# Graph kernel: out-degree sums moved between passes, rows of T in an area of their own, the last group's linear steps ahead of pass six

## The chip, the core and the metric

The kernel runs on one core of a Trainium2 chip. The metric is the time on the device in microseconds; lower is better. TensorE is called PE here, VectorE DVE, ScalarE ACT, GpSimd POOL, and SyncE SP; SP's instructions here are nearly all DMA issues.

## What is computed

Four graph layers in a row on 6250 nodes with 128 features and 200000 edges (src, dst), each followed by `x = layernorm(x + layer(x))`:

```python
# layer 0, three times (l = 0, 1, 2), relu between
t = x @ W[l].T + b[l];  x = (t + segment_sum(t[src], dst)) * 0.5
# layers 1 and 2: GCN with self loops; layer 2 with prelu
out = segment_sum(norm[:, None] * (x @ W)[src], dst) + b
# layer 3: attention over edges, batch norms over all edges
hihj  = concat(x[src], x[dst])
exp_e = exp(silu(bn(hihj @ Wf + bf)));  we = weight[src] * exp_e
a = we / segment_sum(we, dst)[dst]
z = silu(bn(einsum('ed,hdk->ehk', hihj, Wg) + bg))
h = segment_sum(a * z, dst);  out = bn(h) + x
```

The batch norms over edges in layer 3 need sums over the edges of `T[src] + Q[dst]` and of its square (T and Q are x times the two halves of W3, which holds Wg and Wf). They follow from the count of edges for each pair of nodes, and one term needs the out-degree of each node: how many edges start there (`odeg`).

## The kernel before

The nodes are 49 blocks of 128 rows. The kernel counts edges once into a matrix A of counts in device memory (`counts_d`): 49 blocks of target nodes by 49 blocks of source nodes. A word holds two counts: its upper half one of source blocks 0 to 24, its lower half one of source blocks 25 to 48. All segment sums of the layers 0 to 2 are then products with A, in **passes**. Passes one (`FIRST`) and six (`LAST`) go by single blocks (`mm`), with loads called AB, two halves to a block. Passes two to five are grouped (`GROUPED`): 13 groups (`GRP`), ten of 4 target blocks and three of 3.

For each group A comes in seven **chunks** (`CHUNKS`): six of 4 source blocks and a seventh of one. A chunk of a group of four is 1024 KB, of a group of three 768 KB. Three buffers `CA` take the chunks in turn, so that the load of chunk n waits until chunk n-3 is read by all its readers: PE (`chunk_used`), ACT (`chunk_expanded`), which turns the lower halves into floats in `CB`, and DVE, where a sum is taken (`chunk_summed`). The loads are issued by SP in order; `held` and `sums_read` are the counts it waits for. PE goes `highs(0) highs(1) lows_of(0) highs(2) lows_of(1) ... highs(6) lows_of(5)`, each a lot of 8 products (2 for `highs(6)`). The work on the group before stands in between: after `lows_of(0)` the linear step (`group_linear`, L1011), and in pass five also `group_turn` (L1018) and `group_tq` (L1024, products with W3, whose result is T and Q).

**DVE** takes the **out-degree sums**: `chunk_sums` adds up the upper or lower halves of a chunk (TENSOR_REDUCE, L1329) and adds the result to `odeg` (L1330). The table `OD` says in which pass which chunk's halves are summed: for each pass the chunks of the upper halves, then those of the lower halves. Chunks 0 to 2 of the upper halves are summed in pass one. For a group DVE does the sums of chunks 0 and 1, then `finish_group` of the group before (from L1362, L1364 or L1369: bias, relu or layer norm, and `group_split` into a high part, L1338, and the rest, L1340), then the sums of chunks 2 to 6, then in pass five `finish_rows` of the group before.

**Rows of T.** In pass five `finish_rows` writes the rows of T (`TRG`) and Q (`QTG`). TRG shares its place in `TMP` with `YG`, where `finish_group` writes y. POOL copies the high part into HS (L645), then issues the DMAs of T's rows to `table_d` (L647) and Q's to `q_d` (L648), waits for both, and counts `rows_out`. DVE waits for `rows_out` in `finish_group` ahead of y.

**Last group.** The linear step, turn and W3 products of group 12 of pass five stand within block 0 of pass six, ahead of its source blocks 4, 30 and 36. When the rows of group 12 are out, POOL starts the **gather**: for each of 1563 tiles of 128 edges it fetches the rows of T of their source nodes (L662), four sets of 16 tiles in `GS`, and writes them to `rows_d`. The edge loop reads these from there, and stands behind pass six, whose blocks from the third on need Q (`q_in`).

## Time and profile before

| | |
|---|---|
| median of 3 runs | 5065.88 us (5056.94 to 5069.64) |
| the profiled execution | 5055.68 us, its span 5053.8 us |
| PE busy | 3910.6 us, 77% |
| DVE busy | 3272.7 us, 65% |
| ACT busy | 2563.6 us, 51% |
| POOL busy | 1810.3 us, 36% |
| passes two to five | 1417.08 to 2729.6 us of the span |
| gather | 2758.3 to 4921.5 us |

The busy shares are means over stages in which different engines set the pace; what a part costs has to be read in its own stage. All times below are microseconds from the start of the span.

### The profile page before, as it was taken

The numbers are of one execution on the slowest core, as the hardware profiler recorded it, in microseconds if no ns is written. First come the engines' busy times: TensorE is split into PE (matmuls) and PEld (weight loads), VectorE is DVE, ScalarE is ACT, GpSimd is POOL, SyncE is SP. The second block draws the span as 40 slices with busy tenths as digits, with TensorE's granted clock in tenths as the row PEclk, the third lists the DMA queues.
The fourth block names the chain that finished last, engine by engine and source line by source line (L and its number), as shares of the span: only waits on it lengthen the run. The fifth ranks groups of instructions, "written<-read, shape, count | busy, mean of one in ns | idle before, by whom it ended". The sixth has DMA issues, their size and how long they took to land.

```text
span 5053.8 us, 99631 instructions
## 1 busy us (share of the span) xinstructions
PE 3910.6 (77%) x26349; PEld 3254.1 (64%) x26350; DVE 3272.7 (65%) x10813; ACT 2563.6 (51%) x5122; POOL 1810.3 (36%) x1839
## 2 busy tenths in 40 slices
PE   4666555569999989999997996888766666666775
PEld 2222222249988877889887996777755566666764
DVE  6999988775566555322332446888656667666777
ACT  1356788774444434445443444665534444444544
POOL 1000000000000000000002777777777777777770
PEclk8887877689999999999998998999878888888987
DMA  2011222247777766788887996777666666666762
GB/s 83 39 65 78 91 91 104 91 158 258 259 247 266 257 227 219 234 269 265 264 263 219 368 379 199 210 213 210 185 178 181 177 180 192 180 173 181 198 188 90
DMA packets 440519, 976.38 MB, mean 193 GB/s; under 512 B 55380, under 2 KB 159244, under 8 KB 421436
## 3 DMA queue, kind: packets, MB, share of 16 engines
q1 hardware_dynamic: 371619, 755.43, 45.6%
q0 software_dynamic: 67168, 218.56, 14.8%
q8 instruction: 55, 0.90, 0.1%
q10 hardware_dynamic: 1593, 0.80, 0.1%
q14 instruction: 84, 0.69, 0.0%
HBM read 777.04 MB, written 197.54 MB: 193 GB/s over the span
## 4 chain that ended last, share of the span: by engine, by line
POOL 32%; PE 32%; DVE 17%; issue 12%; DMA 3%; ACT 3%; ACTq 1%; SPq 1%; DVEq 0%; POOLq 0%; PEldq 0%; PEld 0%
POOL E L662 31%; PE banks L1040 21%; DVE F L1255 8%; PE banks L967 6%; DVE F L1256 6%; DMA CA<-counts_d 2%; PE banks L938 2%; POOL rows_d L673 1%; ACT banks L710 1%; PE banks L1011 1%; ACT stage L723 1%; PE banks L1072 1%; DMA q_d<-small 1%; ACT stage L721 1%; DMA E<-table_d,IX 1%
## 5 line engine op out<-in xcount | busy, mean ns | idle before, releaser
L662 POOL DMA_INDIRECT E<-table_d,IX x1563 | 1632.3, 1044 | 479.8 <-issue 474.0
L938 PE MATMUL banks<-F 128*128 128x392 bf16 x2368 | 621.1, 413 | 400.1 <-DVE F L1256 255.2
L1123 PE MATMUL banks<-E 128*128 128x129 bf16 x5424 | 427.0, 232 | 516.1 <-DVE E L1493 513.0
L1255 DVE TENSOR_SCALAR F<-F,front 128x392 bf16<-128x392 f16 x2368 | 732.7, 309 | 77.1 <-PE banks L938 70.1
L781 ACT ACTIVATE CB<-CA 128x2048 fp32r<-128x2048 uint16 (+1 forms) x312 | 558.6, 1811 | 392.8 <-DMA CA<-counts_d 371.0
L938 PEld LDWEIGHTS banks<-F 128*128 128x128 bf16 x2368 | 270.4, 114 | 750.8 <-issue 707.3
L1123 PEld LDWEIGHTS banks<-E 128*128 128x128 bf16 x5424 | 349.7, 103 | 585.5 <-DVE E L1493 579.9
L1040 PE MATMUL banks<-CA,HS 128*128 128x512 f32 (+1 forms) x2600 | 646.5, 392 | 47.5 <-DMA CA<-counts_d 47.5
L1040 PE MATMUL banks<-CB,HS 128*128 128x512 f32 (+1 forms) x2496 | 619.6, 388 | 3.3 <-ACT CB L781 3.3
L1040 PEld LDWEIGHTS banks<-CA,HS 128*128 128x128 f32 x2600 | 486.7, 192 | 142.2 <-DMA CA<-counts_d 48.5
L845 ACT ACTIVATE E<-E 128x130 f32<-128x130 f32 x1808 | 574.9, 392 | 0.5 <-DVE E L1527 0.5
L1256 DVE TENSOR_SCALAR F<-F,front 128x128 bf16<-128x128 f16 x2368 | 571.6, 241 | 0.0
L1128 PE MATMUL banks<-E,ident 128*128 128x129 f32 x3616 | 560.7, 302 | 11.5 <-DVE E L1512 10.2
L1135 PE MATMUL banks<-E 128*128 128x130 f32 x3616 | 527.7, 293 | 33.2 <-ACT E L845 33.2
L1040 PEld LDWEIGHTS banks<-CB,HS 128*128 128x128 f32 x2496 | 469.4, 192 | 87.1 <-ACT CB L781 4.0
L1135 PEld LDWEIGHTS banks<-E 128*128 128x128 f32 x3616 | 487.5, 208 | 43.5 <-issue 43.4
L634 POOL CAST HS<-TMP 128x128 f32 (+1 forms) x49 | 20.8, 425 | 1354.7 <-DVE TMP L1271 1354.7
L645 POOL CAST HS<-TMP 128x512 fp32r<-128x512 f32 (+3 forms) x52 | 56.4, 1084 | 1253.3 <-DVE TMP L1338 1253.3
L1128 PEld LDWEIGHTS banks<-E,ident 128*128 128x128 f32 x3616 | 490.2, 210 | 20.2 <-DVE E L1512 19.5
L830 ACT ACTIVATE E<-banks 128x516 f32<-128x516 f32 x452 | 271.4, 601 | 327.8 <-PE banks L1128 309.1
L1493 DVE TENSOR_SCALAR E<-E,node 128x512 bf16<-128x512 uint16 x452 | 194.8, 431 | 358.1 <-DMA E<-dst_d 301.0
L721 ACT ACTIVATE stage<-banks 128x400 f32 (+1 forms) x392 | 249.7, 637 | 342.9 <-PE banks L938 307.9
(235 smaller groups left out, 5296.2 us busy)
## 6 DMA issues: line engine op xcount, KB each, us to landing
CA<-counts_d SPq DMA_DIRECT2D x240, 1024.0 KB, 5.2
E<-rows_d SPq DMA_DIRECT2D x452, 260.0 KB
rows_d<-E POOLq DMA_DIRECT2D x99, 1040.0 KB
AB<-counts_d SPq DMA_DIRECT2D x98, 832.0 KB
counts_d<-stage SPq DMA_DIRECT2D x49, 1600.0 KB, 5.2
AB<-counts_d SPq DMA_DIRECT2D x98, 768.0 KB
E<-dst_d SPq DMA_DIRECT2D x452, 128.0 KB
CA<-counts_d SPq DMA_DIRECT2D x72, 768.0 KB, 4.9
```

What stands on the lines that cost most here:

```text
L662: g.indirect_dma_start(GS[:, t % (GSET * GSETS), :], None, table_d, bass.IndirectOffsetOnAxis(ap=IX[:, t:t + 1], axis=0)).then_inc(g_in[k] ...
L721: act.activation(high16[:, half, :, 2 * k * WIN:2 * (k + 1) * WIN].rearrange("p a h (u d) -> p u (a h) d", u=2), pair[:, :, 0:WB, :], ACT. ...
L781: act.activation(low(q, g, c)[:, 0:size], t[:, 0:size].bitcast(u16).rearrange("p (f k) -> p f k", k=2)[:, :, 0], ACT.Copy).then_inc(chunk_ ...
L845: ins = act.activation(MS[:, h, k, :], ZS[:, h, k, :], ACT.Copy, scale=we[:, h, k:k + 1])
L938: pe.matmul(banks_f[:, ds(e[k], HJ)], ol[:, c * CH + k, :], oh[:, c * CH + k, :], start=False, stop=True, skip_group_check=True).then_inc( ...
L967: ins = pe.matmul(agg[par][:, 0:wide], w, HS[u][:, s, 0:wide], start=(s == 0), stop=(s == NB - 1))
L1040: ins = pe.matmul(sums[:, 0:k * P].rearrange("p (k d) -> p k d", k=k), HS[u][:, s, h * P:(h + 1) * P], words(t, k, w)[:, :, j, :], start=( ...
L1123: ins = pe.matmul(o, OHT[:, k, :], QS[:, p, 0:EDG], start=(k & 1 == 0 and p == 0), stop=False, skip_group_check=True)
L1128: ins = pe.matmul(o, ident[:, :], PAs[:, h, k, :], start=False, stop=(k & 1 == 1), skip_group_check=True)
L1135: ins = pe.matmul(bank[:, 0:ROW], OH[:, h, k, :], MS[:, h, k, :], start=False, stop=True, skip_group_check=True)
L1255: ts(oh[:, n % RING, :], io16, KUL[:, 0, n:n + 1], None, ALU.is_equal)
L1256: ts(ol[:, n % RING, :], io16[:, 0:P], KUL[:, 1, n:n + 1], None, ALU.is_equal).then_inc(onehot_made, 1)
```

## The change

1. Table `OD`: pass two sums the lower halves of chunks 0, 1 and 2 (before: 0, 1), pass three those of 4 and 5 (before: 2 to 5), pass four that of 3 (before: none). The upper halves stay as they are (3 to 6 in pass two).
2. TRG moves from TMP to the start of `small`, over weights and biases of layer 0 that pass five doesn't read; the weights W12 and the biases bias0 change places for that. The wait for `rows_out` moves from `finish_group` to `finish_rows`.
3. POOL issues the two DMAs first and copies the high part into HS after that. Ahead of the gather it also waits for the last split (`group_low_made`), since GS lies over `small`.
4. PE does linear step, turn and W3 products of group 12 ahead of pass six, and no longer within it; ACT does the square root and the copy of the turned X ahead of the first expansion of pass six.

```diff
--- before.py
+++ after.py
@@ -48,7 +48,7 @@
 NLOW = NR // CW
 FIRST, LAST = 1, 6
 GROUPED = (2, 3, 4, 5)
-OD = {2: ((3, 4, 5, 6), (0, 1)), 3: ((), (2, 3, 4, 5)), 4: ((), ()), 5: ((), ())}
+OD = {2: ((3, 4, 5, 6), (0, 1, 2)), 3: ((), (4, 5)), 4: ((), (3,)), 5: ((), ())}
 assert NLOW * CW == NR and GRP[-1][0] + GRP[-1][1] == NB and 6 * CW * 4 * P <= (WB + NR) * 2 * P
 MASK = 4095
 EPS = 1e-5
@@ -109,9 +109,9 @@
         DTG = sb("DTG", [P, 2, NTP], u16)
         IX = sb("IX", [P, NT], u32)
         W0r = small[:, 0:3 * P].rearrange("p (l d) -> p l d", l=3)
-        W12 = small[:, 3 * P:5 * P].rearrange("p (l d) -> p l d", l=2)
+        W12 = small[:, 6 * P:8 * P].rearrange("p (l d) -> p l d", l=2)
         W3 = sb("W3", [P, 2 * EDG], f32)
-        bias0 = small[:, 5 * P:8 * P].rearrange("p (l d) -> p l d", l=3)
+        bias0 = small[:, 3 * P:6 * P].rearrange("p (l d) -> p l d", l=3)
         rowb1 = small[:, 8 * P:11 * P].rearrange("p (l d) -> p l d", l=3)
         biasQ = sb("biasQ", [P, EDG], f32)
 
@@ -128,7 +128,7 @@
         TOPG = TMP[:, 4 * P:4 * P + 4 * EDG]
         YT = TMP[:, 8 * P + 4:9 * P + 4]
         YG = TMP[:, 8 * P + 4:12 * P + 4]
-        TRG = TMP[:, 8 * P + 4:8 * P + 4 + 4 * ROW].rearrange("p (k f) -> p k f", k=4)
+        TRG = small[:, 0:4 * ROW].rearrange("p (k f) -> p k f", k=4)
         QTG = small[:, 11 * P:11 * P + 4 * EDG].rearrange("p (k f) -> p k f", k=4)
         ident = sb("ident", [P, P], f32)
         identr = sb("identr", [P, P], f32r)
@@ -642,14 +642,17 @@
                 w = EDG if q == 5 else P
                 for n, (b0, k) in enumerate(GRP):
                     g.wait_ge(group_top_made, group_no(q, n) + 1)
-                    g.tensor_copy(HS[q & 1][:, b0:b0 + k, 0:w], TOPG[:, 0:k * w].rearrange("p (k f) -> p k f", k=k)).then_inc(group_high_made, 1)
                     if q == 5:
                         g.dma_start(table_d.rearrange("(b p) f -> p b f", p=P)[:, b0:b0 + k, :], TRG[:, 0:k, :]).then_inc(t_row_out, 16)
                         g.dma_start(q_d[b0:b0 + k, :, :].rearrange("b p f -> p b f"), QTG[:, 0:k, :]).then_inc(q_row_out, 16)
+                    g.tensor_copy(HS[q & 1][:, b0:b0 + k, 0:w], TOPG[:, 0:k * w].rearrange("p (k f) -> p k f", k=k)).then_inc(group_high_made, 1)
+                    if q == 5:
                         g.wait_ge(t_row_out, n * 16 + 16)
                         g.wait_ge(q_row_out, n * 16 + 16)
                         g.sem_inc(rows_out, 1)
             g.wait_ge(idx_made, 1)
+            g.sem_inc(gate_g, 1)
+            g.wait_ge(group_low_made, len(GROUPED) * NGRP)
             g.sem_inc(gate_g, 1)
 
             def gather(n):
@@ -814,9 +817,9 @@
                     if p[0] == 5:
                         x_copied(p[1])
             copied(5, NGRP - 1)
-            expand(side(LAST, 0), turn_no(LAST, 0))
             root(5, NGRP - 1)
             x_copied(NGRP - 1)
+            expand(side(LAST, 0), turn_no(LAST, 0))
             expand(side(LAST, 1), turn_no(LAST, 1))
             expand(side(LAST, 0), turn_no(LAST, 0) + 1, order(LAST, 0) + 2)
             with act.Fori(0, NB // 2 - 1) as i:
@@ -1101,9 +1104,10 @@
                     pe.wait_ge(group_high_made, group_no(5, g) + 1)
                 return wait
 
-            pe.wait_ge(group_copied, len(GROUPED) * NGRP - 1)
-            mm(LAST, 0, side(LAST, 0), turn_no(LAST, 0), {0: last_rows(NGRP - 3), 4: lambda: group_linear(5, NGRP - 1), 30: lambda: group_turn(NGRP - 1),
-                                                         36: lambda: group_tq(NGRP - 1), GRP[-2][0]: last_rows(NGRP - 2), GRP[-1][0]: last_rows(NGRP - 1)})
+            group_linear(5, NGRP - 1)
+            group_turn(NGRP - 1)
+            group_tq(NGRP - 1)
+            mm(LAST, 0, side(LAST, 0), turn_no(LAST, 0), {0: last_rows(NGRP - 3), GRP[-2][0]: last_rows(NGRP - 2), GRP[-1][0]: last_rows(NGRP - 1)})
             with pe.Fori(0, NB // 2) as i:
                 for u in (1, 2):
                     mm(LAST, pe.snap(i * 2 + u), side(LAST, u), i + turn_no(LAST, u), {})
@@ -1363,8 +1367,6 @@
                     v.wait_ge(group_lin_done, n + 1)
                     link(tt(y, r, sums, ALU.add))
                 else:
-                    if q == 5 and g:
-                        v.wait_ge(rows_out, g)
                     v.wait_ge(group_lin_done, n + 1)
                     link(tt(y, sums, across(dinv, b0, k), ALU.mult))
                 v.sem_inc(group_lin_read, 1)
@@ -1400,6 +1402,8 @@
 
                 b0, k = GRP[g]
                 v.wait_ge(group_tq_done, g + 1)
+                if g:
+                    v.wait_ge(rows_out, g)
                 cpr(TRG[:, 0:k, EDG:ROW], wn[:, b0:b0 + k].unsqueeze(2))
                 tt(QTG[:, 0:k, :], psQ[:, 0:k, EDG:2 * EDG], along(biasQ[:, :], k, EDG), ALU.add)
                 link(cpr(TRG[:, 0:k, 0:EDG], psQ[:, 0:k, 0:EDG]))
```

On DVE, the second group of pass two (group 1, with the finishing of group 0), before. CA0, CA1 and CA2 are the three buffers; the sums behind the split (L1340) are those of chunks 3, 4, 5 and of the short chunk 6:

```order
L1364 TENSOR_TENSOR TMP<-TMP,banks 128x512 [waits group_lin_done,link_v]
L1372 TENSOR_SCALAR TMP<-TMP 128x512 [waits link_v]
L1338 TENSOR_SCALAR TMP<-TMP 128x512 [waits group_high_made,link_v]
L1340 TENSOR_TENSOR HS0_50<-TMP 128x4x128 [waits group_top_made]
L1329 TENSOR_REDUCE od1<-CA1_56 128x4 [waits chunk_summed,chunk_in1]
L1330 TENSOR_TENSOR odeg<-odeg,od1 128x4 [waits link_v]
L1329 TENSOR_REDUCE od1<-CA2_57 128x4 [waits chunk_summed,chunk_in2]
L1330 TENSOR_TENSOR odeg<-odeg,od1 128x4 [waits link_v]
L1329 TENSOR_REDUCE od1<-CA0_55 128x4 [waits chunk_summed,chunk_in0]
L1330 TENSOR_TENSOR odeg<-odeg,od1 128x4 [waits link_v]
L1329 TENSOR_REDUCE od1<-CA1_56 128x1 [waits chunk_summed,chunk_in1]
L1330 TENSOR_TENSOR odeg<-odeg,od1 128x1 [waits link_v]
```

And after (L1333 is L1329 of before, L1344 L1340):

```order
L1368 TENSOR_TENSOR TMP<-TMP,banks 128x512 [waits group_lin_done,link_v]
L1374 TENSOR_SCALAR TMP<-TMP 128x512 [waits link_v]
L1342 TENSOR_SCALAR TMP<-TMP 128x512 [waits group_high_made,link_v]
L1344 TENSOR_TENSOR HS0_50<-TMP 128x4x128 [waits group_top_made]
L1333 TENSOR_REDUCE od1<-CA0_55 128x4 [waits chunk_summed,chunk_in0]
L1334 TENSOR_TENSOR odeg<-odeg,od1 128x4 [waits link_v]
L1333 TENSOR_REDUCE od1<-CA1_56 128x4 [waits chunk_summed,chunk_in1]
L1334 TENSOR_TENSOR odeg<-odeg,od1 128x4 [waits link_v]
L1333 TENSOR_REDUCE od1<-CA2_57 128x4 [waits chunk_summed,chunk_in2]
L1334 TENSOR_TENSOR odeg<-odeg,od1 128x4 [waits link_v]
L1333 TENSOR_REDUCE od1<-CA0_55 128x4 [waits chunk_summed,chunk_in0]
L1334 TENSOR_TENSOR odeg<-odeg,od1 128x4 [waits link_v]
```

Behind the split there now stands a sum over chunk 2, and those over 3, 4 and 5 follow it.

On PE, the end of pass five and the start of pass six, before; L1040 is the grouped products, L967 those of pass six:

```order
L1011 MATMUL banks<-small_52,TMP 128x128 [waits group_lin_read,group_copied]
L1011 MATMUL banks<-small_52,TMP 128x128 x2
L967 MATMUL banks<-HS1_51,AB_53 128x258 x8
L967 MATMUL banks<-HS1_51,AB_53 128x258 [waits low_expanded]
L967 MATMUL banks<-HS1_51,AB_53 128x258 [waits a_in3]
L967 MATMUL banks<-HS1_51,AB_53 128x258 x10
L967 MATMUL banks<-HS1_51,AB_53 128x258 [waits low_expanded]
L967 MATMUL banks<-HS1_51,BX_54 128x258 x5
L1018 MATMUL banks<-ident,X 128x128 [waits group_x_ready]
L1018 MATMUL banks<-ident,X 128x128 x2
L967 MATMUL banks<-HS1_51,BX_54 128x258 x6
L1024 MATMUL banks<-W3,TMP 128x258 [waits group_xt_copied]
```

And after (L1014, L1021 and L1027 are L1011, L1018 and L1024 of before; L970 is L967):

```order
L1043 MATMUL banks<-CB2_60,HS0_50 128x384 x2
L1014 MATMUL banks<-small_52,TMP 128x128 [waits group_lin_read,group_copied]
L1014 MATMUL banks<-small_52,TMP 128x128 x2
L1021 MATMUL banks<-ident,X 128x128 [waits group_x_ready]
L1021 MATMUL banks<-ident,X 128x128 x2
L1027 MATMUL banks<-W3,TMP 128x258 [waits group_xt_copied]
L1027 MATMUL banks<-W3,TMP 128x258 x2
L970 MATMUL banks<-HS1_51,AB_53 128x258 [waits group_high_made,a_in2,group_low_made,agg_read]
L970 MATMUL banks<-HS1_51,AB_53 128x258 x11
L970 MATMUL banks<-HS1_51,AB_53 128x258 [waits low_expanded]
```

The three steps of group 12 now stand together ahead of the first product of pass six.

## Rows read from the trace of the kernel before

**Rows 1.** The page, chain of work that ended last: shares of the span by line.

```profile
POOL E L662 31%; PE banks L1040 21%; DVE F L1255 8%; PE banks L967 6%; DVE F L1256 6%; DMA CA<-counts_d 2%; PE banks L938 2%; POOL rows_d L673 1%; ACT banks L710 1%; PE banks L1011 1%; ACT stage L723 1%; PE banks L1072 1%; DMA q_d<-small 1%
```

**Rows 2.** The gather's line: count, min/median/max ns, first and last start.

```profile
L662 POOL DMA_INDIRECT E<-table_d,IX x1563: 940/947/6478, 2758.3 to 4921.5; - x196
```

**Rows 3.** Passes two, three, four: length, busy of PE, PEld, DVE, ACT, POOL, PEclk, DMA.

```profile
1417.08:1727.76 310.68, 304.19 (x1471) 258.85 (x1469) 197.57 (x229) 149.65 (x94) 13.91 (x14) 0.99 0.78 261
1727.76:2092.91 365.15, 326.82 (x1471) 274.83 (x1471) 195.80 (x331) 149.99 (x104) 14.09 (x13) 0.93 0.67 221
2092.91:2393.85 300.94, 300.94 (x1472) 257.50 (x1472) 79.35 (x237) 148.00 (x105) 14.06 (x13) 1.00 0.80 267
```

**Rows 4.** Waits of the load queue, pass three: total, times, longest.

```profile
SPq L539 <- DVE odeg L1330: 215.9, 52, 11.3
```

**Rows 5.** Timeline, one group of pass three: start, length, what, idle before.

```profile
1824.45 2.28 DVE L1329 TENSOR_REDUCE od<-CA 128x4 f32<-128x2048 uint16 x1
...
1826.77 0.16 DVE L1330 TENSOR_TENSOR odeg<-odeg,od 128x4 f32<-128x4 f32 x1
...
1832.02 3.46 PE L1040 MATMUL banks<-CA,HS 128*128 128x512 f32 x8 [2.87 <-DMA CA<-counts_d]
```

**Rows 6.** The page, DMA issues: count, size, us from issue to landing.

```profile
CA<-counts_d SPq DMA_DIRECT2D x240, 1024.0 KB, 5.2
...
CA<-counts_d SPq DMA_DIRECT2D x72, 768.0 KB, 4.9
```

**Rows 7.** Timeline, a group of four blocks in pass two.

```profile
1508.61 2.28 DVE L1329 TENSOR_REDUCE od<-CA 128x4 f32<-128x2048 bf16 x1
...
1517.10 2.02 PE L1040 MATMUL banks<-CA,HS 128*128 128x512 f32 x8
```

**Rows 8.** Timeline, a group of three blocks in pass two.

```profile
1716.37 1.75 DVE L1329 TENSOR_REDUCE od<-CA 128x4 f32<-128x1536 bf16 x1
...
1722.54 1.57 PE L1040 MATMUL banks<-CA,HS 128*128 128x384 f32 x8
```

**Rows 9.** Timeline, pass four: a group of four blocks, then one of three.

```profile
2130.51 0.69 DVE L1340 TENSOR_TENSOR HS<-TMP 128x512 fp32r<-128x512 f32 x1
...
2138.57 0.62 PE L1040 MATMUL banks<-CA,HS 128*128 128x512 f32 x2
...
2367.39 0.56 DVE L1340 TENSOR_TENSOR HS<-TMP 128x384 fp32r<-128x384 f32 x1
...
2372.93 0.51 PE L1040 MATMUL banks<-CA,HS 128*128 128x384 f32 x2
```

**Rows 10.** Pass five: two rows of the waits, and a lot of the timeline.

```profile
DVE TMP L1369 <- POOLq L651: 81.4, 10, 9.6
...
PE banks L1040 <- ACT CB L781: 3.3, 2, 2.1
...
2697.77 2.32 PE L1040 MATMUL banks<-CB,HS 128*128 128x384 f32 x8 [2.13 <-ACT CB L781]
```

**Rows 11.** Timeline, the last group; the two rows of DMA are the chain's.

```profile
2729.03 0.56 PE L1040 MATMUL banks<-CB,HS 128*128 128x384 f32 x2
...
2735.56 1.49 PE L1011 MATMUL banks<-small,TMP 128*128 128x128 f32 x6
...
2740.36 0.56 DVE L1369 TENSOR_TENSOR TMP<-banks,dinv 128x384 f32<-128x384 f32 x1 [10.86 <-POOLq L651]
...
2747.64 2.50 PE L1024 MATMUL banks<-W,TMP 128*128 128x258 f32 x6
...
2750.18 0.17 DVE L1185 TENSOR_SCALAR TMP<-wn 128x3 f32<-128x3 f32 x1 [4.29 <-PE banks L1024]
...
2751.94 0.90 POOL L645 CAST HS<-TMP 128x387 fp32r<-128x387 f32 x1 [20.64 <-DVE TMP L1338]
...
2730.55 9.57 DMA q_d<-small
...
2753.52 3.85 DMA q_d<-small
```

## The prediction

> **What bounds the kernel now.** I read the chain of work that ended last first. Its largest share is POOL's gather, 31%, and second the products of the grouped passes on PE, 21% [rows 1]. The reader should see two stretches in series: the passes, in which PE sets the pace, and then the gather of 1563 tiles, issued without a pause from 2758.3 to 4921.5 us [rows 2]. The edge loop behind it follows the gather and ends some 130 us later. So whatever makes the gather start earlier moves the end by as much, as long as the number of tiles and their pace stay, which the change doesn't touch. The question is only when the gather starts: when does group 12 of pass five have its rows in memory?
>
> Then I cut the passes at the first product of each pass and took busy time and length of each. Passes two, three and four do the same products on the same matrix, and last 310.68, 365.15 and 300.94 us [rows 3]. In pass four PE is busy in all of it: 300.94 is what the products cost, and pass three loses 64.2 us against it, pass two 9.7.
>
> The waits of the load queue name the cause: in pass three SP waits 215.9 us for DVE's sums (odeg, L1330), before 52 loads [rows 4]. One group shows how this reaches PE. DVE has ended the split of the group before and starts the sum over chunk 2 at 1824.45; its addition ends at 1826.93. Only then may chunk 5 be loaded into the same buffer (three buffers, so chunk n waits for the reader of n-3). PE comes to it at 1829.1 and waits until 1832.0, 2.87 us, and its next 8 matmuls take 3.46 us, where 8 take 2.02 otherwise [rows 5, 7]. 1832.0 - 1826.9 = 5.1 us is the landing time, and the page has 5.2 us for loads of 1024 KB, 4.9 for 768 KB [rows 6]. 2.9 + 1.4 = 4.3 us per group, and 13 groups make 56 of the 64.
>
> **Pass three, after.** It keeps the sums of chunks 4 and 5 and loses those of 2 and 3. The same group: the split ends at 1824.4, sum 4 at 1826.9. PE's order between two loads' chunks is one lot of 8 from the chunk and one from an expanded one, 1.86 us each (a lot takes 2.02 and overlaps the next), so it reads chunk 4 from 1829.1 - 3.7 = 1825.4 to 1827.3. Sum 5 ends near 1829.5, and PE reads chunk 5 from 1829.1. Neither buffer is held longer than PE holds it, and chunk 5's buffer is released as in pass four. Pass three should come down to pass four's time: **-64.2 us**. I keep +3 as the other bound, for a wait at its first chunks.
>
> **Pass two, after.** It gets one sum more, of 2.28 + 0.16 us and some 0.14 between, 2.6 us. DVE's time isn't what counts (it would be busy 198 + 32 of 311 us [rows 3]); the place does. The sum over chunk 2 comes right behind the split and ahead of chunk 3's. In a group of four blocks that place is 1508.61 [rows 7]: the sum ends at 1511.1, chunk 5 lands 5.2 later at 1516.3, and PE starts on it at 1517.10. It fits, with 0.8 us to spare. The sums behind it each move by 2.6: chunk 3's releases chunk 6 at 1513.7 (needed 1520.8), chunk 4's the next chunk 0 at 1516.3 (lands 1521.5, needed 1524.0). In a group of three blocks the place is 1716.37 and the sum 1.75 us: released 1718.4, landed 4.9 later at 1723.3, and PE wants it at 1722.54 [rows 8]. So 0.8 us of stall in each of three groups: **+2.4 us**. Bounds: 0 below. Above, a landing of 6 us in every group: 10 groups x 0.2 and 3 x 1.9, 7.7 in all, and with PE's slower matmuls behind a stall some 12.
>
> **Pass four, after.** It had no sums; now one over chunk 3 stands behind the split. Four blocks: from 2131.1, ends at 2133.7, then chunk 6 (a quarter of the size) is loaded; PE wants it at 2138.57, 4.9 us later [rows 9]. Three blocks: from 2367.9, ends at 2369.8, wanted at 2372.93, 3.1 us later. The next chunk 0 goes behind it in the queue and has about as much room as it takes. I take 0.3 us for each group of three: **+1 us**, between 0 and 4.
>
> **Pass five, steady part.** The rows of T leave the area that y is written to. Thus the wait for the rows of the group before, at the head of the group's work, falls: 10 waits, 81.4 us on DVE [rows 10]. Most of it costs nothing now; what reaches PE is 3.3 us of waits for ACT's expansion, which stands behind the square root in ACT's order. The 8 matmuls behind the longest of them took 2.32 us [rows 10], and with the two lots behind I count 1.7 us for that. **-5 us**, between -2 and -9 (the loads wait less too). The wait comes back ahead of the write of T's rows. There it asks for a transfer that was issued a whole group earlier (over 18 us ago), so it is covered, except in the last group. POOL's copy into HS now stands behind two DMA issues of 0.75 us; queued behind it is nothing, and who waits for it is DVE's next group, which begins later than that.
>
> **The last group.** Before: the sums end at 2729.6 [rows 11]. PE waits 4.97 us for the first AB half, does 4 products, then the linear step, which ends at 2737.05. DVE waits further, until 2740.36, for the rows of group 11. Then 7.28 us to the first product with W3 (2747.64), 2.50 us for the six, and 8.09 us from there (2750.18) to the gather (2758.27).
> After: the linear step needs only ACT's copy of the sums. With some 0.6 us for that and at most 1.49 for the step, y starts at about 2731.5 (POOL's copy of group 11, 0.90 us behind two issues, is over by then too). Add 7.28 and 2.50: 2741.3. The rows of group 11 must be out now: they landed at 2730.55 + 9.57 = 2740.1, beside the AB loads, and are issued 0.85 us sooner after, so they are covered by 1 to 2 us. Then 8.09, less the 0.84 us of the copy that the first DMA no longer stands behind: gather at 2748.5, 9.7 us sooner.
> Against that: pass six starts its products at 2741.3 instead of 2734.6, so AB loads of its third block now fall on the last rows' way to memory. That way took 3.85 us alone and 9.57 beside loads. I take 1 us of it: **-9 us**, between -4 (all 5.7) and -11 (W3's products at full clock). The new wait of POOL for the last split is over 0.6 us after the DMAs are issued, and hidden by their landing. Pass six itself is not delayed: its third block waits for Q, which is read as soon as the rows are out, and so moves with the gather.
>
> PE is left idle here, behind the sums and again while DVE normalizes. Its matmuls after a stall of 2.87 us were slower by 3.46 to 2.02 [rows 5, 7], and I have therefore used the slow 2.50 us. The Trainium skill says the same in "TensorE: Matmul & The Clock Gate", section "HAM oscillation": idle gaps throw the clock back. By that page the new order is a loss for PE; were the clock kept, the sum would be 1.2 us better.
> A second page speaks against the place of the DMA issues. In "SBUF — State Buffer", section "SBUF: two separate sides", the Trainium skill has GpSimd locked out while a DVE instruction holds the shared ports. The issues now fall beside DVE's subtraction of 0.56 us, and by that page the last group would be 0.5 us later. POOL's copy took its 0.90 us beside that subtraction [rows 11], and I have seen no such hold.
>
> **The sum.** -64.2 + 2.4 + 1 - 5 - 9 = -74.8 us. The profiled execution took 5055.68 us, so 4980.9 for it; its time is 10.2 us under the median of the three runs, 5065.88. Against that median: **4991 us**.
>
> **Rivals.**
> 1. The stall moves instead of going. If the landing in pass two takes 6 to 8 us rather than 5.2, each of its groups stalls 1 to 3 us with slower matmuls behind, and pass four's small groups with it. 15 to 50 us come back: gain 25 to 60, about 5023. For it: 0.8 us of room. Against it: the queue is empty at that point, as chunk 4 was loaded long before, and so it was in pass three's 5.1.
> 2. The end is not set by the gather at the last group, since the edge loop has its own pace, or the last rows land late. Then the 9 us are lost: 5000.
> 3. Slower than before: the chain of buffers. If chunk 2's buffer in pass two and chunk 3's in pass four are held so long that both passes run as pass three does, they cost 64.2 each: 128.4 - 64.2 - 14 = +50, 5116. It decides where a sum ends less than a landing time ahead of PE's turn on the chunk three further; the rooms of 6.0 us (pass two) and 4.9 us for a quarter load (pass four) speak against it.
> 4. The waits are not what holds pass three (the change doesn't do what it says): another 64 us of something stays, and what is gained in pass five is lost in pass two, about 5062. Rows 4 and 5 leave it little.
>
> **Chances.** Forecast 0.74; rival 1 0.14; rival 2 0.05; rival 3 0.04; rival 4 0.03. A measurement can tell about 0.3% (15 us) from no change. Faster by more: 0.93; within: 0.03; slower: 0.04. Bounds of the terms: -64.2 - 9 - 11 = -84, and -61 + 12 + 4 - 2 - 4 = -51, so 4982 to 5015. The profiled run lies 10 us under the median, and the three runs span 13, so I widen below to 4972 and above to 5018.
>
> **What would show it.** Pass three 301 to 304 us long, with PE busy in nearly all of it, and SP's waits for odeg gone from its stall; if it stays over 320, the theory of the buffer is wrong. Pass two 311 to 316: waits of PE for chunk 5 in the groups of three only. Pass four under 305. No wait of DVE at the head of the groups of pass five. From the last sums to the gather 19 to 21 us instead of 28.7, then 2163 us of gather as before; if that stretch is longer by 10 us, the end did not hang on its start.

## The result, and the profile after

The changed kernel takes **4996.13 us**, the median of 4 runs (4992.48 to 5004.04). The kernel before, run beside it, takes 5061.41 (5051.72 to 5069.64). The ratio is 0.9874, with a 95% interval of 0.9851 to 0.9897. The profiled execution took 4992.48, its span is 4990.6; that of before was 5053.8, so the two traces differ by 63.2 us.

The chain that ended last is the one of [rows 1], with the same two lines in front; the row on the wait for q_d is the only one that fell out of the list. Under it stands the gather's line: count, min/median/max ns, first and last start, as in [rows 2].

```profile
POOL E L665 31%; PE banks L1043 21%; DVE F L1259 8%; DVE F L1260 6%; PE banks L970 6%; DMA CA<-counts_d 2%; PE banks L941 2%; POOL rows_d L676 1%; ACT banks L713 1%; PE banks L1014 1%; ACT stage L726 1%; PE banks L1075 1%; ACT stage L724 0%
```

```profile
L665 POOL DMA_INDIRECT E<-table_d,IX x1563: 940/947/7365, 2693.9 to 4858.7; - x196
```

The gather starts 64.4 us sooner and lasts 2164.8 us from its first to its last start, where it was 2163.2. The end is 131.9 us behind its last start. So the time did move with the gather's start. Passes two, three and four, cut as in [rows 3] (length, then busy PE, PEld, DVE, ACT, POOL, PEclk, DMA share, GB/s):

```profile
1416.11:1728.29 312.18, 305.17 (x1471) 258.70 (x1469) 227.81 (x255) 149.35 (x94) 13.90 (x14) 0.99 0.75 259
1728.29:2031.23 302.94, 301.87 (x1471) 257.49 (x1471) 135.47 (x279) 149.72 (x104) 14.07 (x13) 1.00 0.78 266
2031.23:2337.10 305.87, 302.37 (x1471) 257.04 (x1471) 108.49 (x263) 146.69 (x105) 14.08 (x13) 1.00 0.75 262
```

Cut at the same events, the two traces give this:

| stretch | before | after | difference | forecast |
|---|---|---|---|---|
| up to pass two | 1417.08 | 1416.11 | -1.0 | 0 |
| pass two | 310.68 | 312.18 | +1.5 | +2.4 |
| pass three | 365.15 | 302.94 | -62.2 | -64.2 |
| pass four | 300.94 | 305.87 | +4.9 | +1 |
| pass five, to the end of its last sums | 335.74 | 334.67 | -1.1 | -5 |
| last sums to first gather | 28.68 | 22.10 | -6.6 | -9 |
| first gather to the end | 2295.53 | 2296.73 | +1.2 | 0 |

The sum is -63.3, and the forecast's was -74.8.

**Pass three.** The load queue's wait for DVE's sums in the stretch from 1700 to 2040 was 202.1 us in 52 pieces, and is now (total, times, longest):

```profile
SPq L539 <- DVE odeg L1334: 81.3, 37, 5.7
```

Hardly anything of these waits still reaches PE: in pass three it waits twice for a load, 1.1 us in all. A group of pass three in the timeline (start, length, what): DVE makes its two sums behind the split, and PE's lots start without a pause, 1.86 us apart. Where [rows 5] had 2.87 us of waiting and a lot of 3.46 us, every lot takes 2.02 or 2.03.

```profile
1840.23 2.28 DVE L1333 TENSOR_REDUCE od<-CA 128x4 f32<-128x2048 uint16 x1
1841.02 2.03 PE L1043 MATMUL banks<-CA,HS 128*128 128x512 f32 x8
...
1842.81 2.29 DVE L1333 TENSOR_REDUCE od<-CA 128x4 f32<-128x2048 uint16 x1
1842.89 2.02 PE L1043 MATMUL banks<-CB,HS 128*128 128x512 f32 x8
...
1844.75 2.02 PE L1043 MATMUL banks<-CA,HS 128*128 128x512 f32 x8
...
1846.61 2.03 PE L1043 MATMUL banks<-CB,HS 128*128 128x512 f32 x8
```

**Pass four.** The new sum of chunk three (first row) ends at 2310.6. The short chunk 6 has that buffer next, and behind it in SP's queue stand the next group's chunks 0 and 1. PE doesn't wait for chunk 6. It waits for chunk 1, 1.67 us (second row). SP issued chunk 6 at 2310.66, chunk 0 at 2311.13 and chunk 1 at 2312.49. Counted from the end of the group, that is 3.0 us later than in the same group of before for chunk 6 and 1.2 us later for chunk 0; chunk 1 is issued no later (3.8 us ahead of the end, before 3.6). But the three are now under way together, and chunk 1 took 7.09 us to land, where it took 4.21. So it is late by its landing and not by its issue. The three groups of three blocks take 20.30, 19.60 and 20.80 us, where they took 18.75, 18.50 and 18.50. The last sum does this to the first group of pass five too (third row); with it that group takes 25.99 instead of 24.32.

```profile
2308.63 1.75 DVE L1333 TENSOR_REDUCE od<-CA 128x4 f32<-128x1536 uint16 x1
...
2319.63 1.67 PE L1043 MATMUL banks<-CA,HS 128*128 128x384 f32 x8 [1.67 <-DMA CA<-counts_d]
...
2340.56 2.10 PE L1043 MATMUL banks<-CA,HS 128*128 128x512 f32 x8 [1.35 <-DMA CA<-counts_d]
```

**The last group**, which answers to [rows 11]. Its last sums end at 2671.77. y starts at 2673.43, when POOL's copy of group 11 is over. PE has been idle for 5.74 us when the turn comes. The products with W3 take 2.95 us. The last row's way to memory takes 6.65 us, and POOL gathers from 2693.87.

```profile
2673.43 0.56 DVE L1371 TENSOR_TENSOR TMP<-banks,dinv 128x384 f32<-128x384 f32 x1 [1.75 <-POOL HS L648]
...
2679.03 0.90 PE L1021 MATMUL banks<-ident,X 128*128 128x128 f32 x3 [5.74 <-DVE X L1393]
...
2680.51 2.95 PE L1027 MATMUL banks<-W,TMP 128*128 128x258 f32 x6 [0.58 <-ACT TMP L798]
...
2683.50 0.17 DVE L1189 TENSOR_SCALAR small<-wn 128x3 f32<-128x3 f32 x1 [4.52 <-PE banks L1027]
...
2685.48 0.75 POOL L646 DMA_DIRECT2D table_d<-small  x1 [12.09 <-DVE TMP L1342]
```

```profile
2686.23 6.65 DMA q_d<-small
2693.10 0.78 issue
2693.87 1.02 POOL E L665
```

### The profile page after: what moved, and what is told of

It is laid out like the page before. It is cut to its first block, busy times and chain, and to the rows that moved or that the text cites. A ratio compares the mean times of both kernels' runs of the same rounds, so it can differ in the third digit from the quotient of the medians.

```text
span 4990.6 us, 99632 instructions
## 1 busy us (share of the span) xinstructions
PE 3874.5 (78%) x26349; PEld 3224.4 (65%) x26350; DVE 3274.4 (66%) x10813; ACT 2564.4 (51%) x5122; POOL 1806.4 (36%) x1839
## 4 chain that ended last, share of the span: by engine, by line
POOL 33%; PE 31%; DVE 17%; issue 12%; ACT 3%; DMA 2%; ACTq 1%; SPq 1%; DVEq 0%; POOLq 0%; PEldq 0%; PEld 0%
POOL E L665 31%; PE banks L1043 21%; DVE F L1259 8%; DVE F L1260 6%; PE banks L970 6%; DMA CA<-counts_d 2%; PE banks L941 2%; POOL rows_d L676 1%; ACT banks L713 1%; PE banks L1014 1%; ACT stage L726 1%; PE banks L1075 1%; ACT stage L724 0%; PE banks L1027 0%; ACTq L402 0%
## 5 line engine op out<-in xcount | busy, mean ns | idle before, releaser
L1259 DVE TENSOR_SCALAR F<-F,front 128x392 bf16<-128x392 f16 x2368 | 850.0, 518 | 76.4 <-PE banks L941 69.7
L1260 DVE TENSOR_SCALAR F<-F,front 128x128 bf16<-128x128 f16 x2368 | 762.9, 450 | 0.0
L1043 PE MATMUL banks<-CA,HS 128*128 128x512 f32 (+1 forms) x2600 | 634.2, 386 | 17.0 <-DMA CA<-counts_d 16.6
L1043 PE MATMUL banks<-CB,HS 128*128 128x512 f32 (+1 forms) x2496 | 609.6, 383 | 0.0
L1139 PE MATMUL banks<-E 128*128 128x130 f32 x3616 | 517.2, 289 | 41.3 <-ACT E L848 41.2
L634 POOL CAST HS<-TMP 128x128 f32 (+1 forms) x49 | 20.9, 426 | 1353.5 <-DVE TMP L1275 1353.5
L1139 PEld LDWEIGHTS banks<-E 128*128 128x128 f32 x3616 | 477.5, 204 | 50.6 <-issue 50.6
```

The lines of the kernel that those rows point to most:

```text
L1043: ins = pe.matmul(sums[:, 0:k * P].rearrange("p (k d) -> p k d", k=k), HS[u][:, s, h * P:(h + 1) * P], words(t, k, w)[:, :, j, :], start=( ...
L1139: ins = pe.matmul(bank[:, 0:ROW], OH[:, h, k, :], MS[:, h, k, :], start=False, stop=True, skip_group_check=True)
L1259: ts(oh[:, n % RING, :], io16, KUL[:, 0, n:n + 1], None, ALU.is_equal)
L1260: ts(ol[:, n % RING, :], io16[:, 0:P], KUL[:, 1, n:n + 1], None, ALU.is_equal).then_inc(onehot_made, 1)
```

## Experiments

Four sets of runs, each with the kernel before on the same chip. **In the first two sets every kernel, the kernel before too, took some 1690 us more than in the others**: pass six ran from 2370 to 2388 us there, elsewhere 303 to 319. I therefore read their experiments by the stretches up to the gather, and take the whole only as a ratio. Where the same work was traced again, a pass differs by up to 3 us, and pass three with the old table by more (365.15 in the trace of before, 363.09 and 359.75 in two later ones). The stretch ahead of pass two, which no edit touches, ends anywhere from 1411.9 to 1420.8. What pass six did is told at the end.

**1. The table of sums alone.** Everything else as before.

```
-OD = {2: ((3, 4, 5, 6), (0, 1)), 3: ((), (2, 3, 4, 5)), 4: ((), ()), 5: ((), ())}
+OD = {2: ((3, 4, 5, 6), (0, 1, 2)), 3: ((), (4, 5)), 4: ((), (3,)), 5: ((), ())}
```

> The kernel before with the table of the sums alone (the change's part 1). Theory (a chunk's buffer is held by the sum that stands behind the split): pass three falls to 301 to 304 us, pass two rises by 1 to 3, pass four by 3 to 6 in its groups of three only; the whole 54 to 62 us faster than before, ratio 0.988 to 0.9895. Rival (pass three is held by something else, and the tail made the gain): pass three stays over 340 us and the ratio over 0.995.

Measured: 6697.03 us to 6745.93, ratio 0.9927 [0.9912, 0.9942]. Pass two 314.86; passes three and four as their windows:

```profile
1732.57:2036.83 304.26, 301.88 (x1471) 257.48 (x1471) 135.43 (x279) 150.03 (x104) 14.08 (x13) 1.00 0.80 265
2036.83:2341.95 305.12, 302.39 (x1471) 256.98 (x1471) 108.42 (x263) 146.89 (x105) 14.09 (x13) 1.00 0.76 263
```

The first group of pass five takes 25.54. Thus part 1 makes the whole gain of pass three, and also the loss of some 4 us in pass four and 1.2 in the group behind it. Pass two is 4.2 us longer than in the trace of before, more than the 1 to 3 expected. The whole is 48.9 us shorter, not 54 to 62, in a set in which pass six was slow.

**2. The same sums, at another place.** Pass three keeps all four sums. Only that of chunk 2 comes ahead of the last sweep of its group instead of behind it.

```
-                    for c in (0, 1):
+                    for c in (0, 1, 2):
                         chunk_sums
-                    for c in range(2, len(CHUNKS)):
+                    for c in range(3, len(CHUNKS)):
```

> The kernel before, with one thing moved: DVE takes the sum of chunk 2 ahead of finish_group instead of behind it. The table is as before, so pass three keeps all four sums, and DVE does the same work. Theory (what counts is when the buffer is released): chunk 2's buffer is free before PE has read it, and the next sum behind the split, chunk 3's, only holds the short chunk 6; pass three falls from 365 to 301 to 310 us, the whole by 50 to 64 us. Rival (four sums are too much for DVE or for the memory port they share with the loads): pass three stays above 350 us, since DVE's time in it is unchanged.

Measured: 6702.26 us to 6745.93, ratio 0.9939 [0.9924, 0.9954]. Pass three's window:

```profile
1727.69:2042.45 314.76, 305.44 (x1472) 256.27 (x1471) 196.26 (x332) 146.47 (x104) 14.09 (x13) 1.00 0.73 255
```

DVE is busy for 196.26 us, as before (195.80 in [rows 3]), and the pass is 50 us shorter (45 against the shortest of the later traces with the old order). So it was not the amount of DVE's work that held most of pass three, but the time at which one sum let go of its buffer. The pass is still 4.8 us over the upper end of what I expected. The groups of four blocks take 24.5 to 25.3 us; those of three still take 20.9 to 22.9. There the sums over chunks 3 and 4 stand behind the split and hold the buffers of chunk 6 and of the next chunk 0: at the end of one such group the sum over chunk 4 ends at 2015.02, SP issues chunk 0 at 2015.10, and PE waits 0.88 us for it at 2019.60 and 0.88 us more for chunk 1.

**3. The rows' new place and POOL's new order (parts 2 and 3) alone.** The changed kernel with the old table, and with group 12 within pass six as before (ACT's order with it).

```
-            group_linear(5, NGRP - 1)
-            group_turn(NGRP - 1)
-            group_tq(NGRP - 1)
-            mm(LAST, 0, side(LAST, 0), turn_no(LAST, 0), {0: last_rows(NGRP - 3), GRP[-2][0]: ...
+            pe.wait_ge(group_copied, len(GROUPED) * NGRP - 1)
+            mm(LAST, 0, side(LAST, 0), turn_no(LAST, 0), {0: last_rows(NGRP - 3), 4: lambda: group_linear(5, NGRP - 1), ...
```

> The change's parts 2 and 3 alone: rows of T in an area of their own, DMAs ahead of POOL's copy; table of sums and last group as before. Theory: DVE's waits at the head of the groups of pass five go (81 us), PE's 3.3 us of waits for the expansion go, and waits for chunks of 1 to 3 us come; pass five to its last sums 334 to 336 us (335.7 before). In the last group the linear step stands behind the first AB half, but y starts right behind it, at about 7.8 us after the last sums instead of 10.8; so the gather starts 2 to 4 us sooner after the last sums than the 28.7 of before. The whole 0 to 5 us faster, not to be told from none. Rival (this wait was worth much by itself): over 10 us faster.

Measured: 6739.30 us to 6745.93, ratio 0.9989 [0.9980, 0.9998]. The first twelve groups of pass five take 308.34 us, where they took 313.88 in the trace of before: -5.5. But the next experiment's trace, of the same set and with the old place of the rows, has 310.75 for them, so the edit is worth 2.4 to 5.5 us there. To its last sums pass five takes 330.21 us, less than the 334 to 336 expected. From the last sums (2721.07) to the gather (2745.78) it is 24.71, where it was 28.68: -4.0.

**4. The last group ahead of pass six (part 4) alone.** Parts 1 to 3 undone: the edit of experiment 3 the other way round, on the kernel before.

```
-            pe.wait_ge(group_copied, len(GROUPED) * NGRP - 1)
-            mm(LAST, 0, side(LAST, 0), turn_no(LAST, 0), {0: last_rows(NGRP - 3), 4: lambda: group_linear(5, NGRP - 1), ...
+            group_linear(5, NGRP - 1)
+            group_turn(NGRP - 1)
+            group_tq(NGRP - 1)
+            mm(LAST, 0, side(LAST, 0), turn_no(LAST, 0), {0: last_rows(NGRP - 3), GRP[-2][0]: ...
...
-            expand(side(LAST, 0), turn_no(LAST, 0))
             root(5, NGRP - 1)
             x_copied(NGRP - 1)
+            expand(side(LAST, 0), turn_no(LAST, 0))
```

> The change's part 4 alone: linear step, turn and W3 products of the last group ahead of pass six, with rows of T and the wait for them as before. Theory: the linear step is done early and gains nothing, since y waits for the rows of group 11, which land some 10 us after the last sums as before; from the last sums to the gather 27 to 31 us (28.7 before), and the whole within 3 us of before. Rival (it is PE's order that counts, not the wait): 22 to 24 us from the last sums to the gather, 5 to 7 us faster.

Measured: 6743.15 us to 6745.93, ratio 1.0000 [0.9991, 1.0009]. From the last sums (2723.41) to the gather (2754.97) it is 31.56 us, 2.9 more than before. The first two rows say why nothing is gained: y still waits for the rows of group 11, whose way to memory takes 8.75 us, and PE, which has no product of pass six to make meanwhile, stands for 14.02 us. The loss comes behind that. y starts 9.94 us behind the last sums (10.77 before), and its steps and W3's products take 10.07 (9.82). But from there to the gather it is 11.55 us, where it was 8.09: the last rows take 7.30 us on their way (third row, of the chain), where they took 3.85, as pass six's loads now fall on them (experiment 5 takes one such load away).

```profile
2733.35 0.56 DVE L1370 TENSOR_TENSOR TMP<-banks,dinv 128x384 f32<-128x384 f32 x1 [10.04 <-POOLq L651]
...
2738.95 0.90 PE L1018 MATMUL banks<-ident,X 128*128 128x128 f32 x3 [14.02 <-DVE X L1392]
...
2746.76 7.30 DMA q_d<-small
```

Part 4 is a loss by itself (+2.9), part 2 with 3 is a gain (-4.0), and both together are more than their sum (-6.6). Part 4 pays only where the rows are out of y's way: beside experiment 3, y then starts 7.3 us sooner, its steps and W3's products take 1.7 us more (10.07 to 8.34), and the way to the gather 3.0 us more (10.37 to 7.41).

**5. The last rows' way to memory.** The second set: the changed kernel again, and the same with the loads of pass six's third block issued behind the last rows.

> The changed kernel as it is, beside the experiments on their chip. If what was read from one profile of it is its own and not chance: pass two 311 to 313, pass three 302 to 305, pass four 305 to 307, first group of pass five 25.5 to 26, last sums to gather 21 to 23 us; group 11 of pass five (24.8 us there, where pass four's pattern gives 20.7) may differ, since its waits depend on where loads and row writes meet.

```
-            for b in range(3):
+            for b in range(2):
                 load(b, side(LAST, b), turn_no(LAST, b), 1)
             sp.wait_ge(rows_out, NGRP)
+            load(2, side(LAST, 2), turn_no(LAST, 2), 1)
```

> The changed kernel, with SP's AB loads of pass six's third block behind the wait for the last rows instead of ahead of it. Theory (the last rows of T and Q land late beside these loads: 6.65 us where 3.85 were seen alone): they land in 3.4 to 4.2 us and the gather starts 18.5 to 20 us after the last sums (22.1 in the changed kernel). Rival (the landing is long for another reason, such as PE's or DVE's work): landing stays over 6 us, gather at 22 us. The whole 0 to 3 us faster, not to be told from none.

Measured: 6683.75 us to 6745.15 for the changed kernel, ratio 0.9905 [0.9889, 0.9922], and 6683.54 for the other, 0.9909 [0.9892, 0.9925]. From the last sums to the gather it is 21.75 us and then 19.1. The landing is 6.31 us in the one. In the other POOL issues Q's rows at 2691.01 and gathers from 2695.70, 4.69 us later; in [rows 11] it is 4.75 (2753.52 to 2758.27), in the trace of the changed kernel 7.64:

```profile
2691.01 0.75 POOL L648 DMA_DIRECT2D q_d<-small  x1
...
2695.70 1.02 POOL L666 DMA_INDIRECT E<-table_d,IX  x1 [3.42 <-DMA q_d<-small]
```

So the third block's loads are what the last rows share their way with, and that costs some 2.6 us. The whole gains nothing here, as pass six is the slow one in this set.

**6. Pass four's sum at a better place.** The changed kernel, with the sum ahead of the last sweep (as in 2) and chunks 2 and 3 changing passes.

```
-OD = {2: ((3, 4, 5, 6), (0, 1, 2)), 3: ((), (4, 5)), 4: ((), (3,)), 5: ((), ())}
+OD = {2: ((3, 4, 5, 6), (0, 1, 3)), 3: ((), (4, 5)), 4: ((), (2,)), 5: ((), ())}
```

> The changed kernel with two edits: DVE takes the sum of chunk 2 ahead of finish_group, and the table swaps chunks 2 and 3 of the lower halves, so that pass two sums chunk 3's (behind its short split) and pass four chunk 2's (ahead of its long one). As many sums as before. Theory (only a sum that stands behind the split on an early chunk costs): pass four back to 301 to 302 us and the first group of pass five to 24.3, pass two at 310.5 to 312. In all 5 to 8 us sooner at the last sums than the changed kernel. Rival (a sum in pass four costs by its traffic wherever it stands): pass four stays at 305.

Measured: 6678.36 us to 6745.15, ratio 0.9899 [0.9882, 0.9916]. Pass four's window, with DVE busy for as long as in the changed kernel:

```profile
2029.82:2330.81 300.99, 300.99 (x1471) 257.40 (x1471) 110.00 (x264) 148.05 (x105) 14.11 (x13) 1.00 0.81 267
```

The loss of pass four is gone to the last 0.1 us, and the first group of pass five is back at 24.32. From the start of pass two to the last sums it is 1252.99 us, to 1257.67 in the changed kernel: -4.7, a little less than the 5 to 8 expected; pass two takes 312.73, not 310.5 to 312. In the third set the same edit (in experiment 7) leaves pass four at 302.88, to 304.97.

**7. Both, and a gather that waits for T's rows alone.** Q's rows, which the gather doesn't read, are waited for ahead of a later set of tiles. The edits of 5 and 6, and:

```
-            sp.wait_ge(rows_out, NGRP)
+            sp.wait_ge(q_row_out, NGRP * 16)
...
-                        g.wait_ge(q_row_out, n * 16 + 16)
-                        g.sem_inc(rows_out, 1)
+                        if n < NGRP - 1:
+                            g.wait_ge(q_row_out, n * 16 + 16)
+                            g.sem_inc(rows_out, 1)
...
+                    if n == GSETS - 1:
+                        g.sem_inc(gate_g, 1)
+                        g.wait_ge(q_row_out, NGRP * 16)
```

> Both of the above together, and the gather starts when T's rows are out; it waits for Q's rows only ahead of the fourth set of tiles, the first that is written over them. Expected: last sums 5 to 8 us sooner than the changed kernel, gather 17 to 19.5 us after them instead of 22.1; 8 to 13 us faster than the changed kernel where the gather sets the end.

> The changed kernel as it is, beside the two that follow. On a chip where pass six runs beside the gather at 5.9 us a block, both theories expect a ratio of 0.985 to 0.990 to the kernel before; where pass six's products come one in 2.8 us, 0.990 to 0.993, as in the two earlier calls.

> As e8_all: chunk two's sum ahead of the last sweep of its group in pass four, the third block's loads of pass six behind the last rows, and the gather waiting for T's rows alone. Theory (the gather's start sets the end where pass six fits beside it): on a chip with blocks of 5.9 us, 15 to 20 us less than the changed kernel, as the gather starts that much earlier. Rival (something else than the gather's start sets the end): no difference. On a chip where pass six is slow both expect within 6 us of the changed kernel.

Measured in the second set: 6679.69 us, ratio 0.9902 [0.9886, 0.9919]; from the last sums to the gather 17.66. In the third set pass six runs as in the first traces. The changed kernel takes 4997.91 us there (4980.83 to 5001.19), before 5054.67, ratio 0.9892 [0.9873, 0.9912]. This version takes 4978.51 (4972.07 to 4987.84), 0.9858 [0.9836, 0.9879]. The first gather of either, and what POOL waited for ahead of it:

```profile
2687.29 1.03 POOL L665 DMA_INDIRECT E<-table_d,IX  x1 [6.19 <-DMA q_d<-small]
```

```profile
2681.11 1.02 POOL L667 DMA_INDIRECT E<-table_d,IX  x1 [2.04 <-DMA table_d<-small]
```

The gather starts 6.2 us sooner, and the spans are 8.8 apart (4978.9 and 4970.1); the other 2.6 us lie behind the gather's start. I had expected 15 to 20. Of the 17.3 us by which the gather started sooner in the second set (2697.09 to 2679.82), 4.2 were there when pass two began and no edit made them, and I had put them down to the edits as well. 2.1 came in pass two and 0.9 in pass three, 4.1 in pass four, 1.9 in pass five and 4.1 in the last group. In the third set the same account gives 2.1 us in pass four, 1.3 in pass five and 4.2 in the last group, less 1.4 ahead of pass four. The medians are 19.4 us apart, but the intervals of the ratios overlap. So I have two numbers for the gain, 9 and 19 us, and its sign is likely, not certain. Both go the way that the theory of the gather's start says; they don't prove it.

**8. The gather after pass six.** The changed kernel, with one wait more.

```
             g.wait_ge(group_low_made, len(GROUPED) * NGRP)
             g.sem_inc(gate_g, 1)
+            g.wait_ge(agg_done, 2 * NB + 1)
+            g.sem_inc(gate_g, 1)
```

> The changed kernel with one wait more: POOL begins the gather only once pass six's last aggregate is finished. Theory (TensorE's issue starves only while the gather runs): pass six takes 290 to 330 us on any chip, and the whole about 5270 to 5320 us, some 1400 less than the changed kernel where that takes 6680, and 290 more where it takes 4996. Rival (pass six is slow on such a chip by itself, whatever POOL does): pass six still takes about 2200 us there and the whole 8500 or more.

> As e9_gated, on whichever chip comes. If the kernel before takes about 5060 here, both theories expect 5286 again and nothing is told apart. If it takes about 6745, the theory that TensorE's issue starves only while the gather runs expects pass six at 290 to 330 us and about 5300 in all; the rival, that pass six is slow on such a chip whatever POOL does, expects pass six at 2200 us and 7200 or more in all.

Measured: 5286.50 us to 5054.67, ratio 1.0461 [1.0436, 1.0486], and in the fourth set 5290.62 to 5044.90, 1.0478 [1.0411, 1.0545]. The gather's first tile waited for the last aggregate:

```profile
POOL E L667 <- PE banks L972: 300.2, 1, 300.2
```

300.2 us of wait made the kernel 288.6 us longer than the changed one beside it. Those are medians; in the two traces the gather starts 304.2 us later (2991.50 to 2687.29) and the span is 306.8 longer. That is the plainest proof that the end hangs on the gather's start. On pass six it tells nothing new: in both sets pass six ran at its usual pace, beside the gather too, and so this experiment could not tell its two theories apart.

## Why the prediction was right, and where its terms were off

The forecast was 4991, in a range of 4972 to 5018, and the median is 4996. Against the profiled execution it was 4980.9 to 4992.48, 11.6 us too low. The table above splits that; every term had its sign right, and nearly all were a little too good. That the medians come as near as 5 us is in part luck: the forecast adds 10.2 us for the distance of the profiled execution of before from its median, and that of the changed kernel lies only 3.7 under its own.

- **What sets the end**: right. Rival 2 (the end isn't set by the gather) is out: from the first gather to the end it is 1.2 us longer, and a gather that starts 304.2 us later makes the span 306.8 longer.
- **Pass three, -64.2**: measured -62.2. The theory of the buffer is shown by experiment 2, which leaves DVE its work and moves one sum: 45 to 50 of the 64 us go with it. The pass stays 2.0 us over pass four of before; 1.1 of it is time in which PE is idle. Rival 4 is out.
- **Pass two, +2.4**: measured +1.5; PE waits for chunk 5 in the groups of three only, as said, 0.42 and 0.39 us (my 0.8 in each was from a landing of 4.9 us that starts when the sum ends; it was 4.3 and 4.6). The six later traces with the new table and the sums in the same place have pass two at 312.56 to 314.86, so +1.9 to +4.2. In the upper bound, the 0.2 us for each group of four was a slip: 1511.1 + 6 is just PE's 1517.10.
- **Pass four, +1**: measured +4.9, beyond my upper bound of 4. This is the step that failed. I looked at the chunk whose buffer the sum holds, and said in half a sentence that the next chunk 0 "has about as much room as it takes". It has, and chunk 1 behind it hasn't: the late sum puts off chunks 6 and 0, they are under way together with chunk 1, and that lands 7.09 us after its issue instead of 4.21. Pass four's 305.87 is also over the 305 that I had named as a sign. I had also not seen that the sum of the last group falls on pass five's first group, 1.7 us.
- **Pass five, -5**: measured -1.1. The mechanism is as forecast: PE's 3.3 us of waits for ACT's expansion are gone here and in experiment 3, and all of DVE's waits for rows at the head of a group. The size was at the upper end: experiment 3 has 2.4 or 5.5 us for the edit by itself, by which trace it is compared with. Two things took it back: the 1.7 us above, and PE's waits for loads, 5.4 us in all where they were 2.6. The longest is in group 11 of the profiled run (below; 2.14 us, and 2.87 for a lot of 1.56). It isn't in every run: group 11's part, 24.84 us here and 25.78 before, was 22.49 when the changed kernel was run again.

```profile
2635.93 2.87 PE L1043 MATMUL banks<-CA,HS 128*128 128x384 f32 x8 [2.14 <-DMA CA<-counts_d]
```

- **Last group, -9**: measured -6.6, and 22.1 us from the last sums to the gather, where I had named 19 to 21. y came 1.66 us behind the sums (I had 1.9), and 7.08 us lay from there to W3's products (7.28). Two terms were too small. The products took 2.95 us, not 2.50. And from 2683.50 to the gather it was 10.37 us, where I had 7.25 and 1 for the loads beside; the landing of 6.65 us is 2.8 over the 3.85 alone. I had named both the cause and its size (up to 5.7), and took too little of it; experiments 4 and 5 show the cause.
- **Rival 1** (the stall moves instead of going) is what happened in small: 4.9 + 1.5 + 1.7 us came back, of 62. Rival 3 needed that the sums hold the groups of four blocks too, and those ran at 24.5 us in all three passes.

**The clock in the last group.** The granted clock is 0.52 in the 4 us in which W3's products run, and 1.00 in the 10 us behind. In experiment 3, where PE has pass six's products to make until 1.58 us ahead of the turn, it is 1.00 in the same place, and the six products take 1.57 us instead of 2.95.

```profile
2680.00:2684.00 4.00, 3.49 (x11) 2.93 (x12) 0.50 (x2) 4.00 (x4) 0.00 (x0) 0.52 0.70 290
2684.00:2694.00 10.00, 10.00 (x86) 10.00 (x85) 1.82 (x5) 3.60 (x3) 2.14 (x4) 1.00 0.68 207
```

```profile
2736.00:2740.00 4.00, 3.53 (x24) 3.10 (x22) 1.59 (x4) 3.24 (x3) 0.00 (x0) 1.00 0.44 179
```

That is the lower of the two levels (1.2 of 2.4 GHz) behind an idle time of 5.74 us, and it costs 1.4 us in these products; the forecast had put 1.2 on it. The Trainium skill's page "TensorE: Matmul & The Clock Gate", section "HAM oscillation", says that waits of PE between lots of products throw the clock back, and the traces agree. The order of part 4 is still better than the old one: y starts 1.66 us behind the last sums, and 8.96 us behind them in experiment 3, where pass six's first products come in between.

**The shared port.** The last two issues of POOL took 0.75 us each, the first of them at 2685.48 beside DVE's subtraction of 2685.22, no longer than at any other time (0.75 to 0.81 in 13). So the 0.5 us that the forecast named for the issues didn't come. But the forecast was wrong to say that POOL's copy showed no hold either. Before, the copy starts with DVE's subtraction and takes 0.90 us. In the changed kernel the same copy stands behind the two issues, with the subtraction over, and takes 0.52 (first row before, second after; behind the bar busy us and the mean in ns):

```profile
L645 POOL CAST HS<-TMP 128x387 fp32r<-128x387 f32 x3 | 2.7, 899 | 63.1 <-DVE TMP L1338 63.1
...
L648 POOL CAST HS<-TMP 128x387 fp32r<-128x387 f32 x3 | 1.6, 523 | 0.0
```

With four blocks it is 1145 ns and 632. The Trainium skill's "SBUF — State Buffer", section "SBUF: two separate sides", has an exclusive lock between the two engines, and for a DVE instruction with two SBUF inputs, as this subtraction is, only against a GpSimd operation that reads SBUF. The copy reads SBUF and is held by 0.4 to 0.5 us, which agrees; the issues show no hold. Part 3 thus also shortened each of pass five's copies.

## What to carry to other kernels

A reduction on an engine with time to spare isn't free where it reads a buffer that a load waits for: count from its end one landing time, and that for the load that it holds and for each one behind that in the same queue, and take a longer landing where the loads then go out close together (7.1 us instead of 4.2 here). The place of one such sum was worth 45 to 50 us in pass three here, and in pass four a sum cost 5 us or nothing, by its place. Two edits at a pipeline's end should be tried apart as well as together: the new order of the last group lost 2.9 us alone, and gained 2.6 once the rows had their own memory.

## What the runs showed that I had not expected

**Pass six ran at two paces.** In the first two sets all kernels took some 6680 to 6745 us. Where the products of a block come 24 or 25 in 3 us in the first traces, PE issued one in 2.80 us there. It was so for every kernel of a set: that of before took 6745.93 and 6745.15 us in these two, and 5054.67 and 5044.90 in the others; the changed one 6683.75 and 4997.91. PE from the trace of the changed kernel in the second set; its idle time ends with "issue", so PE waited for nothing that the profile shows:

```profile
3001.00 0.38 PE L970 MATMUL banks<-HS,AB 128*128 128x258 f32 x1 [2.42 <-issue]
3003.80 0.38 PE L970 MATMUL banks<-HS,AB 128*128 128x258 f32 x1 [2.42 <-issue]
3006.60 0.38 PE L970 MATMUL banks<-HS,BX 128*128 128x258 f32 x1 [2.42 <-issue]
```

It ends with the gather. POOL's last tile starts at 4878.36 (first row, POOL), and within 6 us PE's products come in lots of 22 to 25 again (the next two, PE). The two windows are the changed kernel's in that set, with and without the gather: PE is busy for 319 of 2180 us at a granted clock of 0.50, then for 171 of 175 at 0.98.

```profile
4878.36 0.94 POOL L665 DMA_INDIRECT E<-table_d,IX  x1 [0.30 <-issue]
...
4884.32 4.11 PE L970 MATMUL banks<-HS,AB 128*128 128x258 f32 x22 [0.34 <-issue]
4888.27 3.05 PE L970 MATMUL banks<-HS,BX 128*128 128x258 f32 x24
```

```profile
2700.00:4880.00 2180.00, 319.42 (x883) 245.24 (x883) 55.30 (x171) 51.53 (x36) 1534.83 (x1658) 0.50 0.38 110
4880.00:5055.00 175.00, 171.42 (x1411) 171.26 (x1412) 84.28 (x261) 83.44 (x56) 1.09 (x2) 0.98 0.82 276
```

The gather itself kept its pace (median 946 ns a tile there and 947 in the first trace; 2181 and 2165 us from first to last start), and DMA was busy for 0.38 of the time, less than where all went well (0.99 in 2700 to 2990 us of the changed kernel's first trace). Passes two to five, which have no gather beside them, were as long as ever. So in those sets PE issued its products slowly while POOL issued the gather, by what is not shown. The loading of instructions doesn't show as the cause: from 2720 to 2900 us the queues for instructions moved 2 packets in the slow trace of the changed kernel and 2 in its first. It isn't the chip alone: the fourth set ran on a chip with the same number as the second, and had the fast pace. Nor is it the kernel. Experiment 8 was to show whether pass six is fast there once the gather waits, and met the fast pace both times, so this stays open. What it means for a reader: in such a set the end is set by pass six and the edge loop behind it. Pass six took 2370 to 2373 us in the four traces of the second set, whether the gather started 6.5 or 10.7 us behind its first product. So what the passes gain shows in the whole (5.4 us in experiment 6), and what only brings the gather forward does not (0.2 us in experiment 5; and experiment 7's version, whose gather starts 6.9 us ahead of experiment 6's, takes 6679.69 to 6678.36).

**Lengths in the profile that are no cost.** In the first trace of the changed kernel two instructions of DVE ahead of pass two have mean lengths of 518 and 450 ns (L1259 and L1260, 2368 times each), and 308 and 240 when the same kernel was run in the third set. But these records overlap one another. Around 330 us a pair starts every 0.39 us in that trace and in the one of before, with lengths of 0.69 and 0.62 in the one and 0.30 and 0.24 in the other. The whole stretch, from the first such instruction to the last, takes 1011.5 us, to 1011.4 before and 1008.1 in the third set. So the engine's pace was the same and only the recorded lengths grew; I have no cause for that.
